# TensorE sums the experts ahead of the chunk's output in the last three chunks of a full step

## Time and profile before

| | |
|---|---|
| median of three executions | 1549.94 us |
| the profiled execution's own time | 1547.93 us |
| its span on the core | 1546.2 us |
| TensorE busy (matmuls) | 1418.8 us, 92% of the span |
| VectorE busy | 1075.2 us, 70% |
| ScalarE busy | 863.1 us, 56% |
| GpSimd busy | 275.4 us, 18% |
| share of TensorE in the chain that ended last | 59% |
| mean granted TensorE clock | 0.952 of full |
| the chunk loops' last three chunks in the three full steps | from 176, 319 and 461 us |

### The profile page before, as it was taken

How to read it: one execution, slowest core, us unless ns; L and a number is a source line. 1 busy time by engine, 2 the same in 40 slices (tenths; PEclk the granted TensorE clock), 3 DMA queues, 4 the chain that set the end, 5 groups by cost and what they waited for, 6 DMA issues and landing times.

```text
span 1546.2 us, 21289 instructions
## 1 busy us (share of the span) xinstructions
PE 1418.8 (92%) x7543; PEld 635.6 (41%) x7543; DVE 1075.2 (70%) x2056; ACT 863.1 (56%) x1751; POOL 275.4 (18%) x409
## 2 busy tenths in 40 slices
PE   6998998899788988999999999999999999985786
PEld 3655665575556553222223232233322333322353
DVE  7766568738755577888887879888888888843023
ACT  6554235415531322677777777777777767773142
POOL 2211121102111203000000110501104111043452
PEclk9989899889979988999999999999999999998898
DMA  4080000200010922111101111011101100000135
GB/s 122 9 197 14 1 1 14 100 1 1 29 72 1 165 100 100 36 22 21 22 2 22 39 22 22 26 25 40 22 14 26 26 1 2 1 5 26 42 99 172
DMA packets 47343, 64.45 MB, mean 42 GB/s; under 512 B 9730, under 2 KB 34893, under 8 KB 45398
## 3 DMA queue, kind: packets, MB, share of 16 engines
q1 hardware_dynamic: 44166, 58.84, 14.9%
q0 software_dynamic: 3072, 4.25, 0.8%
HBM read 33.08 MB, written 32.03 MB: 42 GB/s over the span
## 4 chain that ended last, share of the span: by engine, by line
PE 59%; DVE 6%; ACT 2%; issue 2%; POOL 1%; DMA 1%; DVEq 0%; ACTq 0%; POOLq 0%
PE ps L591 57%; DVE smax L2046 2%; PE ps L584 1%; ACT space L1417 1%; POOL expert_in L1609 1%; DVE st L1759 1%; ACT space L1438 0%; PE ps L940 0%; DVE x_all L1777 0%; ACT space L1459 0%; PE ps L1072 0%; DMA shift_rows<-shiftT 0%; DMA space<-expert_in 0%; DVE x L1995 0%; DVE mv L1764 0%
## 5 line engine op out<-in xcount | busy, mean ns | idle before, releaser
L591 PE MATMUL ps<-space 128*32 128x512 f32 (+5 forms) x4608 | 846.7, 476 | 33.5 <-DVE space L1901 14.2
L2046 DVE TENSOR_REDUCE smax<-ps 128x1 f32<-128x1024 f32 x512 | 605.1, 1219 | 119.1 <-PE ps L591 113.0
L1417 ACT ACTIVATE space<-ps 128x512 f32<-128x512 f32 x1024 | 555.2, 595 | 211.1 <-PE ps L591 210.5
L591 PEld LDWEIGHTS ps<-space 128*32 128x32 f32 (+5 forms) x4608 | 248.6, 109 | 604.7 <-ACT space L1417 328.9
L1510 POOL TENSOR_SCALAR eps_sum<-mv 128x4 f32<-128x4 f32 x32 | 7.3, 229 | 615.1 <-DVEq L1766 614.6
L1272 ACT ACTIVATE btok<-ps 128x128 f32<-128x128 f32 x32 | 8.9, 277 | 148.4 <-PE ps L591 68.1
L591 PE MATMUL ps<-ones,ident 128*128 128x512 bf16 x271 | 73.1, 423 | 15.9 <-POOLq L1613 12.3
L591 PE MATMUL ps<-w_exp,space 128*128 128x128 f32 x512 | 81.5, 311 | 0.0
L591 PEld LDWEIGHTS ps<-w_exp,space 128*128 128x128 f32 x512 | 69.8, 213 | 16.1 <-issue 15.9
L1860 DVE SCALAR_TENSOR_TENSOR space<-space,conv_w 128x512 f32<-128x512 f32 x96 | 71.1, 750 | 2.3
L1609 POOL DMA_INDIRECT expert_in<-space,slot x64 | 62.9, 982 | 36.3 <-issue 19.3
(11 more groups left out here) (252 smaller groups left out, 1487.7 us busy)
## 6 DMA issues: line engine op xcount, KB each, us to landing
q_rows<-space SPq DMA_DIRECT2D x24, 256.0 KB, 2.4
k_rows<-space SPq DMA_DIRECT2D x24, 256.0 KB, 2.9
space<-k_rows SPq DMA_DIRECT2D x16, 384.0 KB, 5.3
space<-q_rows SPq DMA_DIRECT2D x16, 384.0 KB, 7.0
expert_out<-x_all SPq DMA_DIRECT2D x2, 2048.0 KB, 21.3
space<-expert_out SPq DMA_DIRECT2D x4, 1024.0 KB, 8.6
v_rows<-space SPq DMA_DIRECT2D x4, 668.0 KB, 3.6
space<-v_rows SPq DMA_DIRECT2D x4, 668.0 KB, 6.6
```

Source lines behind the costliest of these rows:

```text
L591: return nc.tensor.matmul(out, lhsT, rhs, start=first, stop=last)
L1417: nc.scalar.activation(prob[:, QUAD * (step % PROB_SETS) + unit % QUAD, :], bank(STB + unit % 2), ACT.Exp)\
L2046: v.tensor_reduce(smax[:, N % 2, i:i + 1], ps[:, b0:b0 + 2, :].rearrange("p k n -> p (k n)"), AX.X, ALU.max).then_inc(S.s_max, 1)
```

## The change

In chunks 5, 6 and 7 (`c > HT`) of a step that has both m and p, TensorE issues `chunk_out(m, c)` behind the `keep_clock` matmuls and the chunk's sums, and not ahead of them. In every other chunk and step the place is the old one. No instruction is added or taken away, and no other engine's program changes.

```diff
@@ -896,7 +896,7 @@
                         gates_turned(p)
                         if m is not None:
                             keep_clock(OUTB, 5)
-                    if m is not None:
+                    if m is not None and (p is None or c <= HT):
                         chunk_out(m, c)
                     if p is not None:
                         if c == 0:
@@ -914,6 +914,8 @@
                                 score_pair(PAIRS_IN_SUMS[k])
                             if k == E - 1:
                                 keep_clock(OUTB, 3)
+                        if m is not None and c > HT:
+                            chunk_out(m, c)
                 if m is not None:
                     mix_out(m, 1)
                 if p is not None:
```

## The result

The changed kernel takes 1609.74 us (median of 4, 1608.56 to 1618.38) against 1547.68 us for the kernel before (median of 4, the three from above and one more). The ratio is 1.0398, with a 95% interval of 1.0368 to 1.0429. It is slower by 62 us; 33.6 us were forecast, and 1598 us was the upper end of the range. The sign and the waits were right; how often the waits would bring the low clock was not. A time at the granted clock 0.50 is called a low spell here, as in the prediction.

The account below looks back on a forecast made before the run. Between chunks a short relay and TensorE's dense work were taken to bound the loop in turn; 23.1 us of stalls plus 10.5 us of low clock, 33.6 us on 1547.93, gave 1581 us, range 1561 to 1598.

Parts of the forecast that it names:

- Chunk 5's stall: Before chunk 5's first sum, TensorE idles 1.87 us instead of doing the output, which then costs 1.48 us behind the sums.
- Chunk 6's stall: Before chunk 6's first sum, TensorE idles 2.52 us because VectorE's gate, waiting for output 5, delays the relay 2.23 us.
- Chunk 7: Output, gate and squares stand bare before mix_out(m, 1): 4.17 us in two steps, 3.60 us in the third.
- Sum of the stalls: Over the three full steps, stalls of 7.88 us twice and 7.31 us once, 23.1 us in all.
- No cover behind the step: Behind each full step the chain goes on without slack, so all of the step's delay was let through.
- The clock: One new spell at 1.2 GHz per full step, in chunk 6, adding 10.5 us.
- the upper bound of two per step: At most two new low-clock spells in every full step, 6 x 3.5 = 21 us; 1592 us in all, chance 0.18.
- The price of a spell: A low-clock spell slows three gate rows with their sums by 1.18 us each, 3.5 us.
- Rival 1: In the full steps, stalls come without new low-clock spells: 1571 us, chance 0.22.
- Rival 3: Five old low-clock spells in and behind the steps go away and none come: 1553.5 us, chance 0.05.
- Rival 4: Stalls are absorbed behind the step by 7 to 8 us of slack: 1548 us; chance 0.07 together with rival 5.
- Rival 5: TensorE takes the ready output while the sum waits, so nothing changes: 1548 us; chance 0.07 together with rival 4.

Follow-up runs that it names:

- the moved gate: The filled kernel with VectorE's gate for chunks 4 and 5 moved to the end of chunk 6, 3 fewer fill matmuls there: 1567.25 us, ratio 1.0130.
- the filled kernel: The changed kernel with keep_clock matmuls put into the new TensorE waits of chunks 5 to 7: 1568.69 us against 1548.66, ratio 1.0117.

## Why the prediction was right and where it went wrong

- *Chunk 5's stall*, 1.87 us forecast: 1.96, 1.92 and 1.84 us. Right, and the output's 1.48 us to the digit.
- *Chunk 6's stall*, 2.52 us: 2.51 us in all three steps. The gate held `chunk_carry` as forecast, shown by the moved gate (0.64 us against 0.75).
- *Chunk 7*: sums wait 2.15 us in two steps and 0.95 us in the third, where there is no `input_norm`; `mix_out(m, 1)` waits 2.47 us for the squares in each. Right.
- *Sum of the stalls*, 23.1 us: 22.9 us by the waits, and 23.5 us by the filled kernel's stretches.
- *No cover behind the step*: right, the third step's end moved by the whole growth (1606.8 - 559.7 = 1047.1 us are left behind it, against 1546.2 - 498.7 = 1047.5 before).
- *The clock*, "I take one per step", 10.5 us: this step failed, and with it the upper bound of two per step, 21 us. The mechanism was right, the count was not: nine new spells begin in the three stretches (four, two and three), where three were taken and six allowed. TensorE's work there took 34.0 us longer. The price of a spell was nearly right: 34.0 / 9 = 3.8 us against 3.5, and about as much comes back where chunk 4's old wait is filled (11.5 / 3 = 3.8 us a step by the medians, 10 / 3 = 3.3 by the ratio). The new spells last 3.4 to 23.9 us, 10.2 on average, and chunk 4's old ones 10.2, 13.7 and 10.2. Nine at the old price would have made it 1547.9 + 23.1 + 31.5 = 1602.5 us; of the rest, 4 us lie between the second and the third step, and no run looks into them.
- *Where the bound came from*: by the prediction's own working four waits in a step are new or longer, and its upper end let only two of them act. It also says that no row shows a wait of 2.5 us in this loop. The trace of before has two, in chunk 2 of the second full step and in chunk 1 of the third:

```profile
290.83 0.69 PE L591 MATMUL ps<-space 128*64 128x128 f32 x4 [2.99 <-DVE space L1901]
...
424.74 0.44 PE L591 MATMUL ps<-space 128*64 128x128 f32 x4 [2.50 <-DVE space L1901]
```

  Behind both the granted clock is 0.50, from 290.6 to 297.4 and from 427.2 to 434.0. Of the seven waits of 1.1 us or more for another engine in these loops five are followed by the low clock, chunk 4's three among them; behind chunk 3's two of 1.49 us (155.22 and 439.86) it stays up. So a new wait was more likely to bring the low clock than not, and the length of a wait alone does not decide.
- *Rival 1* (the clock holds) is what the filled kernel shows, 1568.69 us where 1571 was given. *Rival 3*: no new spells is what fell; of the old ones chunk 4's stayed (6.8, 13.7 and 13.7 us), and those behind the steps shrank from 6.8 us each to none, 3.4 and 3.4, as it had allowed. *Rival 4* fell with the sign. *Rival 5* fell too: in chunk 6 the output's operands were ready by 191.43 while the sum ahead of it kept TensorE idle until the gate rows at 194.28. The Trainium skill (PSUM — Partial Sum Buffer, "Engine vs sequencer instructions") states this order, and the trace agrees.
- The Trainium skill (TensorE: Matmul & The Clock Gate, "Why this matters for your kernels") asks for no idle gaps of TensorE between bursts of matmuls, but names only gaps that are longer than any new wait of this change. By that no new spell would come, and the time would be rival 1's 1571 us. The trace does not agree: waits of 0.95 to 2.51 us stand at the falls to 0.50, and filling them takes the spells away. The measurement decides.

## What to carry to other kernels

An independent piece of work between a producer's start and its consumer is cover; before moving it behind the consumer, read what that consumer waits for, and who waits for the piece moved. Price a new TensorE wait twice, as a wait and as the clock it may bring down for the dense work behind it; here the second was one and a half times the first (34.0 us against 22.5 in the three stretches). Count every new wait as one that may bring it, and look for the nearest waits in the whole trace, not in the chunk at hand. Where a wait can't be had away, cheap matmuls sized to end inside it are worth trying: 5 per step gave 0.65% on the old order, and 109 in all took back 41 of 62 us on the new one.

## What the runs showed of the hardware

By the mean granted clock the low time in the three stretches rose from 2 x (0.02 x 38.8 + 0.03 x 39.0) = 4 us to 2 x (0.20 x 55.1 + 0.30 x 59.8 + 0.26 x 56.6) = 87 us. So a low spell cost 34.0 / 83 = 0.41 us per us. A dense sum loses 1.18 of 2.54 us, 0.46 per us, and part of the low time is waiting (from 375.40, 17.05 of 20.10 us are busy). Behind a step, where the projections at the full clock wait for ScalarE (0.69 and 0.32 us), part of the gain is lost.

Waits of like size did not act alike. The three of 1.8 to 2.1 us in chunk 5, moved alone, added 3.8 us of busy time; chunk 7's, moved alone, added 19.2 us (2.15 us twice, 0.95 once, 2.47 three times). What decides whether a wait brings the low level, and how long that lasts, stays open.
